# Moving layer 1's preparation into layer 0 of a two-layer attention kernel, with a reordered tail of layer 0

## What is computed

```python
# layer 0: 8 heads of 32, each with two softmaxes over 16 features (differential attention)
scores = einsum('bqhif,bkhif->ibhqk', q, k) * scale      # 512 x 512 per head and batch
att = softmax(scores)[0] - diff_weight * softmax(scores)[1]
s = rmsnorm(att @ v) * norm_w @ Wo.T + bo, times (1 - diff_weight)
g = silu(top-2 gated low-rank product)                   # 8 experts, rank 16
# layer 1: 16 heads of 64, attention over the 8 entries of the batch axis for each token position
attn = softmax(q k^T + q k_dist^T);  out = attn v + attn v_dist;  s = out @ W_out.T + b_out
g = silu(sqrt((x cos(theta + theta_noise))^2 + (x sin(phi + phi_noise))^2))
```

## Time and profile before

| | us |
|---|---|
| median of 3 runs | 1353.73 |
| lowest and highest of them | 1352.47, 1357.69 |
| the profiled execution's own time | 1348.0 |
| its span in the profile | 1346.2 |
| TensorE busy | 1224.7 (91%) |
| VectorE busy | 957.1 (71%) |
| ScalarE busy | 680.0 (51%) |
| GpSimd busy | 604.7 (45%) |

### The profile page before, as it was taken

One profiled execution on the slowest core, in us unless ns is written; L12 is line 12 of the kernel. 1 busy time (PEld: TensorE's weight loads), 2 busy tenths in 40 slices (PEclk: granted clock), 3 DMA queues, 4 the chain that ended last, 5 costly groups with the idle time before them and its releaser, 6 DMA issues. The chain is left out here.

```text
span 1346.2 us, 30256 instructions
## 1 busy us (share of the span) xinstructions
PE 1224.7 (91%) x10752; PEld 771.5 (57%) x10752; DVE 957.1 (71%) x2084; ACT 680.0 (51%) x1293; POOL 604.7 (45%) x618
## 2 busy tenths in 40 slices
PE   3889999999999999898769899999999999999997
PEld 2333344444444444343358687777878777786875
DVE  2766776777778777776375968688696868869675
ACT  2356666666665666666343344344344434434442
POOL 2165667676766767766642313132231313223131
PEclk8598999999999999999869999999999999999999
DMA  4634453554444354450240010010101001010000
GB/s 125 145 80 88 98 117 88 118 119 93 99 91 106 87 126 91 99 117 8 99 175 32 3 47 3 10 41 1 49 2 49 2 10 41 1 49 2 32 3 17
DMA packets 57205, 86.27 MB, mean 64 GB/s; under 512 B 8064, under 2 KB 38016, under 8 KB 56832
## 3 DMA queue, kind: packets, MB, share of 16 engines
q1 hardware_dynamic: 57088, 84.58, 25.8%
HBM read 50.47 MB, written 33.55 MB: 62 GB/s over the span
## 5 line engine op out<-in xcount | busy, mean ns | idle before, releaser
L821 DVE TENSOR_REDUCE negmax<-s_bank 128x1 f32<-128x512 f32 x512 | 330.9, 680 | 76.2 <-PE s_bank L555 75.7
L969 POOL TENSOR_TENSOR room<-room 128x512 f32<-128x512 f32 x256 | 318.8, 1276 | 130.2 <-ACT room L685 130.2
L685 ACT ACTIVATE room<-t_bank 128x512 f32<-128x512 f32 x512 | 284.8, 597 | 79.7 <-PE t_bank L565 74.5
L555 PE MATMUL s_bank<-kst,qst 48*128 48x512 f32 x512 | 214.1, 488 | 15.6 <-DMA kst<-park 13.4
L565 PE MATMUL t_bank<-qst,kst 50*128 50x512 f32 x512 | 207.0, 468 | 17.0 <-ACT room L685 12.8
L565 PEld LDWEIGHTS t_bank<-qst,kst 50*128 50x128 f32 x512 | 83.6, 188 | 140.2 <-ACT room L685 82.0
L1724 POOL TENSOR_TENSOR room<-rt,apart 128x512 f32<-128x512 f32 x32 | 42.2, 1339 | 234.6 <-DVE rt L1533 234.6
L578 PE MATMUL a_bank<-room,v 128*32 128x512 f32 x1024 | 137.6, 611 | 0.2
L1709 POOL TENSOR_TENSOR ex<-ex,rc 128x256 f32<-128x256 f32 x64 | 41.9, 655 | 188.6 <-DVE rc L1561 188.6
L1576 DVE STREAM_TRANSPOSE pt<-ex 32x256 f32<-32x256 f32 x256 | 111.0, 434 | 10.1 <-POOL ex L1709 3.6
L1262 PE MATMUL pr<-xt_h,win_h 128*128 128x512 f32 x256 | 105.6, 413 | 0.0
(11 more groups left out here) (251 smaller groups left out, 2282.1 us busy)
## 6 DMA issues: line engine op xcount, KB each, us to landing
park<-qk_h SPq DMA_DIRECT2D x128, 128.0 KB, 2.4
qst<-park SPq DMA_DIRECT2D x64, 192.0 KB, 3.8
kst<-park SPq DMA_DIRECT2D x64, 192.0 KB, 4.3
park<-qk_l SPq DMA_DIRECT2D x64, 128.0 KB, 2.4
room<-in_x SPq DMA_DIRECT2D x8, 512.0 KB, 4.5
xr<-in_x SPq DMA_DIRECT2D x8, 512.0 KB, 5.3
xb<-x SPq DMA_DIRECT2D x8, 512.0 KB, 4.4
xr<-x SPq DMA_DIRECT2D x8, 512.0 KB, 3.7
```

What stands on the lines that cost most here:

```text
L555: pe.matmul(s_bank[S_BANK[w]][:, :], qst[slot][rows, j, c * P:(c + 1) * P], kst[slot][rows, j, :], start=True, stop=True).then_inc(m.s_don ...
L685: act.activation(probs[:, c, j, :], t_bank[w % 2][:, :], ACT.Exp, scale=SCALE0).then_inc(m.exp_done, 1)
L821: dve.tensor_reduce(negmax[:, i_par, 2 * odd + j, c:c + 1], s_bank[S_BANK[w]][:, :], X, ALU.max, negate=True).then_inc(m.max_done, 1)
L969: add = pool.tensor_tensor(sums[:, pair, h, :], probs[:, 2 * pair, h, :], probs[:, 2 * pair + 1, h, :], ALU.add)
```

## The change

It has these parts:

1. `W_in` gets a place of its own (24 KB per partition) and is loaded in 8 pieces of 384 columns, each after a `fill_stacks` in batches 1 and 6 (four each).
2. The angles, noises and four small tables are loaded by SyncE at the start of the last batch (8 transfers). The 15 steps of `less_turns` run one at a time on VectorE in half-steps 1 and 2 of the last batch (`TRIG`).
3. In the last half-step of the last batch the denominators come straight from the probabilities: 4 groups of 4 matmuls (`last_denominators`) in place of GpSimd's two `add_pair` and 2 groups of 4.
4. `win_h` is written over stack slots 0 to 2 by ScalarE in the tail (three pieces), `win_l` over probs by VectorE in the tail (three pieces). `gk` is computed in the tail ahead of OT.
5. `LAST_JOBS` is reordered, and GpSimd adds the maps tile by tile.
6. x1's first tile has its own semaphore, and layer 1's first rows are loaded in the tail behind it; layer 1 no longer waits for all stores at the meeting point.
7. In layer 1's start the weights' and angles' preparation is gone, apart from sine, cosine and their parts; `ones` products come ahead of the transposes.

The diff, cut to its core:

```diff
+TRIG = tuple((1, w) for w in (0, 1, 2, 3, 4, 8, 9, 10)) + tuple((2, w) for w in (0, 1, 2, 3, 8, 9, 10))
+WIN_PIECES = 8
+WIN_BATCHES = (1, B - 2)
-LAST_JOBS = [("TD", B - 1, 0)] + [("TA", B - 1, t) for t in range(QT)] + [("OT", B - 1, 0), ("OT", B - 1, 1),
-             ("ZT", B - 1, 0)] + [("WF", B - 1, t) for t in range(QT)]
+LAST_JOBS = [("ZT", B - 1, 0), ("TA", B - 1, 0), ("TA", B - 1, 1), ("TD", B - 1, 0), ("TA", B - 1, 2), ("TA", B - 1, 3),
+             ("OT", B - 1, 0), ("OT", B - 1, 1)] + [("WF", B - 1, t) for t in range(QT)]
...
+    def load_weights(self, sp, io, n):
+        cols = slice(n * 3 * H1 * D1 // WIN_PIECES, (n + 1) * 3 * H1 * D1 // WIN_PIECES)
+        sp.dma_start(self.win[:, :, cols],
+                     io["win"].rearrange("(k p) n -> p k n", p=P)[:, :, cols]).then_inc(self.w_load, 16)
...
     def load_first(self, sp, io):
+        sp.dma_start(self.wqn, io["wqn"].rearrange("(h p) c -> p h c", p=P)).then_inc(self.b_load, 16)
...
+    def low_weights(self, dve, n, part):
+        dve.wait_ge(self.w_high, n + 1)
+        cols = slice(part * H1 * D1, (part + 1) * H1 * D1)
+        dve.tensor_tensor(self.win_l[:, :, cols], self.win[:, :, cols],
+                          self.win_h[:, :, cols].bitcast(F32), ALU.subtract).then_inc(self.w_low, 1)
...
# SyncE, layer 0
             def body(b):
+                if isinstance(b, int) and b >= B - 1:
+                    sp.wait_ge(m.xt_psum, KC * B)
+                    shared.load_angles(sp, io1)
                 for hf, v_, kind, i, k in slots(b):
                     if kind == "PROJ":
                         park_parts(i)
                         fill_stacks(i, k)
+                        if isinstance(b, int) and b in WIN_BATCHES:
+                            shared.load_weights(sp, io1, HALF * WIN_BATCHES.index(b) + hf)
...
             sp.wait_ge(m.ta_psum, QT * B)
             shared.load_last(sp, io1)
-            for t in range(QT):
+            for t in range(2):
                 store_x1(B - 1, t)
-            for stored in m.x1_stored:
-                sp.wait_ge(stored, 16 * B * QT // 2)
+            sp.wait_ge(shared.x1_stored_even, 16 * (QT // 2) * (B - 1))
+            sp.wait_ge(shared.x1_stored_first, 16)
+            shared.load_tokens(sp, x1_dram)
+            for t in range(2, QT):
+                store_x1(B - 1, t)
...
# TensorE, layer 0
+            def last_denominators(c):
+                pe.wait_ge(m.exp_done, HALF * UNITS * B - UNITS + 4 * c + 4)
+                for h in range(HG):
+                    mm = pe.matmul(d_bank[BLK * h:BLK * h + BLK, :], pick[:, HALF - 1, :], probs[:, c, h, :],
+                                   start=False, stop=(c == 3))
...
+                            if last and hf == HALF - 1 and w >= 7:
+                                last_denominators(w // 4 - 1)
+                            if last and (hf, w) == (HALF - 1, UNITS - 1):
+                                value_step(b, hf, 2)
...
+            last_denominators(3)
+            value_step(B - 1, HALF - 1, 3)
...
+                if (kind, k) == ("OT", 0):
+                    pe.wait_ge(m.td_psum, B)
+                    pe.wait_ge(m.d_evac, B)
+                    pe.wait_ge(shared.b_load, 16)
+                    pe.wait_ge(shared.k_load, 16 * shared.K_LOADS)
+                    (16 products of wqn and kdx into d_bank, as L1288)
...
# ScalarE, layer 0
+            act.wait_ge(shared.w_load, 16 * WIN_PIECES)
+            high_weights(2)
+            side("DEV", B - 1, 0)
             values_out(HALF * B - 1, HALF - 1)
-            side("DEV", B - 1, 0)
+            high_weights(0)
             for n, (kind, i, k) in enumerate(LAST_JOBS):
                 side(kind, i, k, last_banks[n % len(last_banks)])
+                if (kind, k) == ("ZT", 0):
+                    high_weights(1)
                 if (kind, k) == ("TA", QT - 1):
                     for t in range(QT):
                         side("SQ", i, t)
+                    act.wait_ge(shared.g_psum, 1)
+                    (copy of gk)
...
# VectorE, layer 0
+                        if last and (hf, w) in TRIG:
+                            shared.less_turns(dve, TRIG.index((hf, w)))
...
+            dve.wait_ge(m.a_done, 16 * B)
+            dve.wait_ge(m.d_done, SUMS * B)
+            shared.low_weights(dve, 0, 2)
+            (TD, four TA)
+            for n, part in ((1, 0), (2, 1)):
+                shared.low_weights(dve, n, part)
+            (four WF)
...
# GpSimd, layer 0
-                add_pair(b, 3, 0)
+                if not last:
+                    add_pair(b, 3, 0)
-            add_pair(B - 1, 3, 1)
-            add_maps(B - 1)
+            for k in range(QT):
+                add_last_maps(k)
...
# VectorE, layer 1
-            low_weights(0, 2)
             norm_stats(0)
-            low_weights(1, 0)
+            (8 products for kdb)
             normalise(0)
             for kc in range(KC):
                 low_parts(0, kc, (misc, fin)[kc])
-            low_weights(2, 1)
```

More of the change, by code:

```diff
@@ L219, in less_turns @@
[L219 to L226, removed]
-            dve.scalar_tensor_tensor(turns, ang, -1.0, ang, op0=ALU.mult, op1=ALU.max).then_inc(self.trig, 1)
+        elif op:
+            dve.wait_ge(self.trig, step)
@@ L581, in value_step @@
                 mm.then_inc(m.a_done, 1)
+            def last_denominators(c):
[3 more added lines that the diff above has]
+                                   start=False, stop=(c == 3))
+                if c % 2:
+                    mm.then_inc(m.d_done, 1)
+                else:
+                    stand_alone(pe, m.pe_passed)
             def denominators(b, hf, pair):
-                first, last = (hf, pair) == (0, 0), (hf, pair) == (HALF - 1, PAIRS - 1)
+                first = (hf, pair) == (0, 0)
+                last = (hf, pair) == (HALF - 1, PAIRS - 1) and not (isinstance(b, int) and b >= B - 1)
                 if first:
@@ L656, in _ @@
             over_batches(pe, body, 2, 2)
-            for step in range(16 - LAG, 16):
-                value_step(B - 1, step // 4, step % 4)
-            for pair in range(PAIRS):
-                denominators(B - 1, HALF - 1, pair)
+            last_denominators(3)
+            value_step(B - 1, HALF - 1, 3)
             wait(pe, *drained(*prev))
@@ L666, in _ @@
                     pe.wait_ge(*drained(*LAST_JOBS[n - len(last_banks)]))
+                if (kind, k) == ("OT", 0):
[3 more added lines that the diff above has]
+                    pe.wait_ge(shared.k_load, 16 * shared.K_LOADS)
+                    for hp in range(HP):
+                        for kc in range(KC):
+                            mm = pe.matmul(d_bank[:, kc * P + 2 * NREL * hp:kc * P + 2 * NREL * (hp + 1)],
+                                           shared.wqn[:, hp, kc * P:(kc + 1) * P],
+                                           shared.kdx[:, :, :].rearrange("p a b -> p (a b)"), start=True, stop=True)
+                    mm.then_inc(shared.g_psum, 1)
                 if kind == "WF" and k == 0:
@@ L1283, in free_pr @@
                 return pr[:, n % 2, :]
-            pe.wait_ge(m.b_load, 16 * BLOADS)
-            for hp in range(HP):
-                for kc in range(KC):
-                    pe.matmul(o_ps[:, 0, kc * P + 2 * NREL * hp:kc * P + 2 * NREL * (hp + 1)],
-                              wqn[:, hp, kc * P:(kc + 1) * P], kdx[:, :, :].rearrange("p a b -> p (a b)"),
-                              start=True, stop=True)
-            for kc in range(KC):
-                transposes(0, kc, (misc, fin)[kc])
+            pe.wait_ge(m.k_load, 16 * KLOADS)
             pe.wait_ge(m.kdb_ok, HP)
@@ L1297, in _ @@
             mm.then_inc(m.g_psum, 1)
-            pe.wait_ge(m.g_ok, 2)
+            for kc in range(KC):
+                transposes(0, kc, (misc, fin)[kc])
             pe.wait_ge(m.w_low, 1)
```

206 lines of the change are left out of this document (122 added, 84 removed).

## The result

The changed kernel takes 1369.99 us (median, 1366.39 to 1373.78) against 1353.1 us for the kernel before (1348.56 to 1357.69): ratio 1.0125, interval 1.0076 to 1.0174. It is slower by 1.25%, and the forecast was 1352. The profiled execution took 1372.79 us with a span of 1371.0 us; before it was 1348.0 with 1346.2. The two profiled executions lie 24.8 us apart where the medians lie 16.9 apart, because the one of before was 5.1 us under its median and the changed one 2.8 over. Where the 24.8 us of span went is read off three marks: the end of the last exponential E, the start of layer 1's first R, and the end.

The account below looks back on a forecast made before the run. TensorE's in-order stream was taken as the bound in layer 0's body, with VectorE about a quarter free. Body +9.3, tail -8.2, layer 1's start -3.7 and clock +0.8 gave -1.8: from 1353.7 to 1352 us, range 1343 to 1360.

Parts of the forecast that it names:

- From V on layer 1 is the same before and after.: Layer 1 behind V's start: the change adds and saves nothing there, apart from a clock term of +0.8 us.
- Body of layer 0: Layer 0 up to the last exponential: added pieces, loads, angle steps and denominators cost +9.3 us.
- the pieces: Weight pieces in batches 1 and 6: their transfers delay `ml`, 1.8 us in each batch, +3.6 us together.
- Angle steps: Fifteen steps on VectorE in the last batch: partly in its free time, +3.5 us, between 0 and 16.
- Last denominators: Last half-step of layer 0: two new matmul groups in TensorE's stream cost +2.0 us to the last exponential.
- Rival 3: Last batch, half-steps 1 and 2: VectorE becomes the bound, steps cost +15 instead of +3.5, 1364 us; chance 0.12.
- Tail: From the last exponential to layer 1's start: +26.5 us instead of +34.7, a saving of 8.2 us.
- Layer 1's start: Stretch from layer 1's beginning to V: 16.7 us against 20.4, a saving of 3.7 us.
- `wqn` landed: Tail: this load, issued at +3.6 us and first in its queue, takes 5.2 us and lands at +8.8.
- `gk`'s products: Tail, ahead of OT: 16 products take 4.7 us, between 3.5 and 7.0, ending at +13.5.
- rival 2: Tail: `wqn` lands late and `gk`'s products run at the low clock throughout, +6 on the forecast, 1358 us; chance 0.13.
- the clock's +0.8: V's first matmuls in layer 1 may run at the lower clock level: +0.8 us, 0 to 1.7.

Follow-up runs that it names:

- a_gap: Changed kernel with 24 unused semaphore increments on TensorE ahead of layer 1 and 832 unused bytes ahead of the room of probabilities: 1354.25 us, ratio 1.0002.
- a_pad24: Changed kernel with 24 unused semaphore increments on TensorE ahead of layer 1's first wait: 1355.93 us, ratio 1.0033.
- a_pad4: Changed kernel with 4 unused semaphore increments on TensorE ahead of layer 1's first wait: 1370.71 us in one execution.
- a_late: a_pad24 with all fifteen angle steps moved behind units 8 to 15 of the last half-step, two at a unit: 1351.64 us, ratio 0.9975.
- a_den: a_pad24 with the last half's denominators as in the kernel before and 24 increments more: 1360.48 us, ratio 1.0043.
- a_best: a_late with `gk`'s products behind WF, weight pieces behind the maxima, and VectorE's second and third low parts of the weights later: 1343.23 us, ratio 0.9935.
- a_best2: a_best with VectorE's third low part behind the cosines' low parts and the first tokens' transposes ahead of the `ones` products: 1342.79 us, ratio 0.9919.

## Why the prediction was wrong

The forecast was 1352 us, same as before; measured 1.25% slower.

**The step that failed** is "From V on layer 1 is the same before and after." Its instructions are the same, and their place is not. In place of nothing, this term was +20.0 us. Padding takes 16.0 of them away (657.5 to 641.5 us): 11.2 are the five waits, and by an estimate from the rows 4.7 are the low clock behind two of them (twice 1.23 us of R, some 2.2 us of V's first matmuls at 0.43 instead of 0.23). Of the other 4.0 V's pitch is 2.6. Taking the seams away with 24 increments took the ratio from 1.0125 to 1.0033, which is 0.92 points of the 1.25, and putting seams into the kernel before made it 0.8 and 1.6% slower. What was left out of the sum was a resource that the diff changes without naming it: the position of a loop in the code.

**Body of layer 0.** Forecast +9.3, measured +13.8 in the changed kernel's execution. One execution is a poor measure of it: E is at 669.5, 670.4 and 667.8 us in a_gap, a_pad24 and a_pad4, which have the same body, and at 658.4 in both padded versions of before, so +9 to +14. And the three executions of before's body were each the quickest of their kernel. What is left of the difference of the medians when the steadier two columns are taken off is +6 (the changed kernel and a_gap) to +10 us (a_pad24), an estimate, and the forecast lies in that range. The terms: for the pieces +3.6 was forecast; the wait for `ml` grew by 1.35 us in batch 6 (0.76 in the earlier trace rows to 2.11 in a_late) and by 1.0 in batch 1 (0.93 to 1.97), not by 1.8 each, and moving the pieces moved the last TD mark by 2.1 us and E by 0.6. Angle steps +3.5, measured 2.9 and 2.6 by the medians on one chip. Last denominators +2.0, not seen in the body (a_den).

**Rival 3** (VectorE the bound, 0.12) was right about the place and wrong about the size: VectorE was full from 620 to 640 and one step took 2.63 us, but the fifteen took 15.5 us, 1.03 on average and so under the 1.2 at which the rival sets in, and the price was some 3 us and not 15. The rule about the lock of VectorE and GpSimd agrees with these traces: in a_best one product of GpSimd took 2.77 us instead of 0.72 beside a low part that had begun 0.54 us earlier, and the four additions of maps took 4.82 us with the low parts beside them and 2.77 in a_best, where these wait.

**Tail.** Layer 1's start was forecast at E + 26.5 and measured at E + 30.7. `wqn` landed 5.5 us after its issue (the list of transfers) where I took 5.2. The mis-sized term is `gk`'s products: 4.7 taken, 6.72 measured at the low clock throughout (rival 2's second half), and their start at E + 9.6 instead of + 8.8. WF came at + 18.85 instead of + 15.7; moving the products away gave the 3.7 us back.

**Layer 1's start.** From the layer's start to V 15.1 us (716.93 - 701.8) against 16.7 forecast, and the clock's +0.8 came out: V's fifth matmul starts 1.75 us behind its first, before 1.01. a_best2 does not show that putting the transposes ahead of `ones` gains anything: its 3.3 us lie in front of layer 1 (last residual at E + 22.5 instead of 25.9), and from the last residual to first R it takes 12.2 us where a_best takes 12.1. The transposes still wait, for `xn`.

Without the seams the changed kernel stands at 1.0033 (a_pad24) or 1.0002 (a_gap) of the kernel before. On the 1353.7 us of the forecast that is 1358 or 1354 us where the sum said 1352: the rest of the sum was off by 2 to 6 us, inside the range of 1343 to 1360.

## What to carry to other kernels

Where a loop sits in its engine's code is part of the kernel: when a change adds or removes instructions ahead of a loop, look at the seam after the jump for an "issue" wait, and try pads of several lengths in an idle stretch before judging the change (24 increments took the seams away here, 4, 21 and 45 moved them or made them). Work moved into "free" time of an engine should go where that engine is free at the moment, not on average: the same fifteen steps cost some 3 us in half-steps 1 and 2 and nothing behind unit 8 of the last one. And where a wait in front of a small product is hidden, as with `gk`, it should be moved together with what hides it.

## What was not expected of the hardware

A jump back to a head with 1, 3, 5 or 13 matmuls left ahead of the end of its 16.3 KB of instructions stops TensorE for 2.6, 2.4, 2.2 or 1.5 us on average (13.1, 12.0, 11.2 and 7.4 us over five seams), with 23 left not at all. On crossing a block's end the Trainium skill, "Runtime: NRT & Kernel Launch", section "Instruction fetch mechanics", says that the cost is "mostly hidden"; in straight code the traces agree (a_pad24 has no "issue" wait of TensorE's matmuls over 0.9 us in the whole execution), right behind a jump they do not. And the granted clock fell behind the stall: in the changed kernel to 0.50 behind two of the five seams, where R's remaining 11 matmuls took 2.72 us instead of 1.49.
